# Order of ScalarE's squares and VectorE's norms in two interleaved streams of a transformer kernel

## The reference

```
x = x + softmax_over_rows(n(x) n(x)^T) n(x)            # n = layernorm
x = x + ffn(n(x))                                      # two layers
x = x + weighted_values(n(x))
x = x + ffn(n(x))                                      # the same two layers

def layer(x):                                          # one of the two, 8 heads of 64, windows of 64
    q, k, v = split(shift(x) @ wqkv)
    q = q / |q| * qs ;  k = k / |k| * ksc              # per head
    q, k = q * cos * scale + rot(q) * sin * scale, k * cos / scale + rot(k) * sin / scale
    x = x + local_attention(8 * q, k, v) @ wo          # this window and the one before
    h = layernorm(shift(x)) @ w1 + b1 ; a, g = split(h)
    return x + (a * gelu(g)) @ w2 + b2
```

## Time and profile before

| | us |
|---|---|
| median of three runs (1572.09 to 1573.59) | 1572.35 |
| the profiled execution, its own time | 1571.71 |
| its span, first to last instruction | 1569.9 |

### The profile page before, as it was taken

How to read it: one execution, slowest core, us unless ns; L and a number is a source line. 1 busy time by engine, 2 the same in 40 slices (tenths; PEclk the granted TensorE clock), 3 DMA queues, 4 the chain that set the end, 5 groups by cost and what they waited for, 6 DMA issues and landing times.

```text
span 1569.9 us, 46462 instructions
## 1 busy us (share of the span) xinstructions
PE 1445.2 (92%) x18975; PEld 1121.2 (71%) x18975; DVE 1300.5 (83%) x1692; ACT 1231.8 (78%) x1834; POOL 897.2 (57%) x626
## 2 busy tenths in 40 slices
PE   5999997889999999999998767989999999999998
PEld 3777874777777777777776554777777777777776
DVE  6777757888899999898885866988998998988884
ACT  4876867788888888888885857788888888888884
POOL 4334104666666666766761645776666666667761
PEclk9999999999999999999999878999999999999999
DMA  4312003675566756656650003666666565565562
GB/s 115 111 51 91 11 7 70 132 128 117 119 122 126 115 118 127 122 123 120 120 105 20 0 8 71 134 132 111 122 127 120 117 123 122 124 119 123 113 110 67
DMA packets 359855, 157.46 MB, mean 100 GB/s; under 512 B 299410, under 2 KB 335836, under 8 KB 359644
## 3 DMA queue, kind: packets, MB, share of 16 engines
q1 hardware_dynamic: 359644, 154.51, 49.0%
HBM read 27.29 MB, written 6.29 MB: 21 GB/s over the span
## 4 chain that ended last, share of the span: by engine, by line
PE 54%; ACT 20%; DVE 11%; issue 5%; DMA 4%; SPq 4%; POOL 1%; DVEq 0%; POOLq 0%; ACTq 0%
PE PS L199 8%; PE PS L201 7%; PE PS L200 7%; PE PS L852 6%; DMA t<-t 4%; PE PS L827 4%; PE PS L871 4%; ACT t L1059 3%; PE PS L834 3%; PE PS L860 3%; ACT t L1143 2%; PE PS L914 2%; DVE t L1256 2%; ACT L1200 2%; ACT L1143 2%
## 5 line engine op out<-in xcount | busy, mean ns | idle before, releaser
L1432 POOL TENSOR_TENSOR t<-t 128x1024 f32<-128x1024 f32 x128 | 308.2, 2408 | 207.8 <-DVE t L1262 207.4
L1438 POOL TENSOR_TENSOR t<-t 128x512 f32<-128x512 f32 x256 | 320.5, 1274 | 150.5 <-DVE t L1272 150.2
L1272 DVE TENSOR_TENSOR t<-t 128x1024 f32<-128x1024 f32 x128 | 208.5, 1629 | 0.1
L199 PE MATMUL PS<-wqh,HH 128*128 128x512 f32 x384 | 179.8, 468 | 21.0 <-DVE t L1262 10.9
L1256 DVE TENSOR_REDUCE t<-t 128x16 f32<-128x1024 f32 x128 | 156.0, 1219 | 33.3 <-ACT t L1059 32.2
L1291 DVE TENSOR_REDUCE t<-PS 128x8 bf16<-128x1024 f32 x128 | 156.1, 1220 | 16.9 <-PE PS L801 16.7
L1279 DVE TENSOR_TENSOR t<-t,PS 128x1024 bf16<-128x1024 f32 x128 | 155.1, 1212 | 9.9 <-ACT PS L1079 9.6
L1079 ACT CAST PS<-t 128x1024 f32<-128x1024 bf16 x128 | 130.2, 1017 | 41.6 <-DVE t L1291 32.2
L852 PE MATMUL PS<-t 128*64 128x65 f32 x4096 | 147.5, 224 | 13.0 <-DVE t L1325 13.0
L1262 DVE SCALAR_TENSOR_TENSOR t<-t,PS 128x1024 f32<-128x1024 f32 x128 | 155.0, 1211 | 0.6 <-ACT t L1066 0.6
L201 PE MATMUL PS<-wqh,HL 128*128 128x512 f32 x384 | 152.8, 398 | 0.0
(11 more groups left out here) (242 smaller groups left out, 3411.9 us busy)
## 6 DMA issues: line engine op xcount, KB each, us to landing
t<-t SPq DMA_DIRECT2D x254, 130.0 KB, 2.4
t<-turns SPq DMA_DIRECT2D x128, 128.0 KB, 2.8
t<-yT SPq DMA_DIRECT2D x108, 128.0 KB, 2.4
t<-t SPq DMA_TRANSPOSE x304, 3.4
t<-in_c_rope SPq DMA_DIRECT2D x32, 128.0 KB, 2.2
turns<-t SPq DMA_DIRECT2D x32, 128.0 KB, 1.9
t<-in_L_attn_a_x SPq DMA_DIRECT2D x4, 512.0 KB, 7.0
t<-yT SPq DMA_DIRECT2D x16, 127.8 KB, 2.6
```

The source lines that it names most:

```text
L199: e.matmul(o, ah, bh, start=not more, stop=False, skip_group_check=True)
L1272: e.e.tensor_tensor(BL.ta[i % 2].rearrange("p (x h) d -> p x h d", x=2), BL.qn.rearrange("p (x h) d -> p x h d", x=2), cos.to_broadcast([1 ...
L1432: e.e.tensor_tensor(BL.tc.rearrange("p (x h) d -> p x h d", x=2), BL.qn.rearrange("p (x h) d -> p x h d", x=2), sin.to_broadcast([128, 2, ...
L1438: e.e.tensor_tensor(tv[:, :, 32 * s:32 * s + 32], tv[:, :, 32 * s:32 * s + 32], BL.tc[:, :, 32 * (1 - s):32 * (1 - s) + 32], ALU.add).then ...
```

## The change

ScalarE: in every step but A, `squares(s)` is issued in front of `copy_result(s - 4)`; in A the order stays. VectorE: in G, `norms(s)` is issued in front of `rope(s - 1)`; in the others it stays behind. `normed` has one more wait, that the rotation's product of the tile before is done (`la_ta`), since otherwise nothing would keep it from overwriting `qn` early. No instruction is added or removed, and TensorE, GpSimd and SyncE keep their lists.

```diff
@@ layers_act, the loop over s
                 if on(3):
                     exps(s - 3)
+                behind_gelus = chunk_at(s, 13) is not None
+                if on(0) and not behind_gelus:
+                    squares(s)
                 if on(4):
                     copy_result(s - 4)
...
-                if on(0):
+                if on(0) and behind_gelus:
                     squares(s)
@@ layers_dve, normed(i)
                 e.wait_ge(S.la_tc, hi(i - 1) + 1)
+                e.wait_ge(S.la_ta, hi(i - 1) + 1)
@@ layers_dve, the loop over s
                 if on(2):
                     low(s - 2)
+                if on(0) and chunk_at(s, 12) is not None:
+                    norms(s)
                 if on(1):
                     rope(s - 1)
...
-                if on(0):
+                if on(0) and chunk_at(s, 12) is None:
                     norms(s)
```

## The result

| | before | after |
|---|---|---|
| median of the runs (4 and 4), us | 1572.97 (1572.09 to 1576.93) | 1557.09 (1554.27 to 1559.34) |
| ratio, 95% interval | | 0.9893 (0.9868 to 0.9918) |
| profiled execution, its own time | 1571.71 | 1558.34 |
| its span | 1569.9 | 1556.5 |
| first-layer round, us | 36.22 | 35.55 |

The forecast was 8.7 us faster; the change made it about 16 faster.

What follows compares the result with a forecast made beforehand. TensorE was taken as nearly the bound, its stalls the only gain. 16 rounds by 0.55 (8.8), ten rounds (0.5) and transposes (-0.6) made 8.7 us off 1571.71: 1563.0, as median 1563.6; range 1555.5 to 1573.

Steps and rivals of the forecast that it cites:

- both stalls of TensorE: TensorE's waits for the exps (0.44 us) and for VectorE's gated product (about 0.5), some 0.9 us a round.
- the collision: In ten second-layer rounds GpSimd's sine's product starts 0.86 us later and overlaps VectorE's cosine product, which ends 0.86 later.
- A, by G: Earlier ln, rounding and exps one step before end TensorE's stall of 0.44 us at the values; it gains 0.40.
- Bank 7 in C: TensorE's product from bank 7 waits for ScalarE's later copy; another 0.04 us lost there a round.
- The slower rival: The late copy holds TensorE's bank 7 products and the first steps: 8.7 us slower, 1581; chance 0.13.
- Its other term: In the first steps of each stage project_out (L871) passes the copy's delay on: 14 by 0.47 us, 6.6.
- B: VectorE's norms no longer wait for the squares, so TensorE's gather wins 0.19 us of its stall of 0.5.
- The second layer: Ten rounds in which late GpSimd work leaves only 0.09 less 0.04 us a round: 0.5 in all.
- The transposes (0.6): TensorE's waits in front of L816 for a transpose by L709: 0.1 us taken off, six times.
- The first 12 steps (0): Steps outside full rounds, project_out (L871) behind the later copy, norms earlier: taken as 0, between -0.3 and +0.47 us a step.
- GpSimd takes it back everywhere: Rival: GpSimd's late additions and chunk work collide in all 26 rounds, gaining only 1.3 or 2.6 us: 1570.5; chance 0.23.
- More than that: Rival: no collision in the ten rounds and a gain in the first steps, 14.3 and 2 more: 1556; chance 0.12.

Runs made afterwards that it cites:

- moving the residual: The whole change, with GpSimd's addition of the residual one step later, behind the sine's product instead of in front of it: 1555.44 us, ratio 0.9889.
- The change once more: The changed kernel run again without any edit: 1557.19 us, ratio 0.9904 to the kernel before.

## Why the prediction was right in direction and too small in size

The mechanism held: both stalls of TensorE that the forecast named were there and shrank by the path that it gave, and the loss and the collision that it expected came too. What was off is the size of one term, the reach of the collision, and a round that it took for one like the others. The runs give each term its size.

- **A, by G: right.** Forecast 0.44 won in A, less 0.04 for bank 7 in G; measured 0.44 (9.35 to 8.91) and 0.04 (10.03 to 10.07). Each link of the chain came within 0.05 us: ln 0.81 for 0.76, rounding 0.65 for 0.63, product 1.22. That the rounding would be bounded by GpSimd's additions held as well. What I hadn't worked out is how little of it is needed: ScalarE's exchange alone brings the exps 0.31 forward and 0.31 of the 0.38 that G's exchange is worth.
- **Bank 7 in C: right.** Forecast 0.04, measured 0.02 to 0.04 (C 8.15 to 8.17, and the round without it 35.55 to 35.51). The slower rival put 0.15 and 0.12 on this mechanism; it is there, at a quarter of that. (Its other term counts 14 steps outside full rounds; by the 94 exchanged steps less 78 in full rounds they are 16.)
- **B: the term was mis-sized**, 0.19 for 0.30. I took the row's idle time in front of the norms for what could be won. VectorE's instructions start some 0.08 before the end that the row of the one before gives (576.77 starts inside 575.18 + 1.67 = 576.85), so an instruction that need not wait wins the idle time and this overlap, 0.27. 0.03 is unexplained. Over 24 rounds this term is 2.6 us, and it explains the first-layer round: 0.55 forecast, 0.67 measured.
- **The second layer: the collision came, its reach was overrated.** It is there (2.46), and moving the residual gave back what it took (35.87 to 35.54). The forecast had it take all of A's gain and half of B's through `add_out`, `reduce_maxima` and `normed`, and let 0.05 a round stay. The runs show 0.38: B kept all of its 0.31, and A kept 0.11. The step that failed is "comes out about 0.1 late": `add_out` was not 0.1 late but 0.08 early. TensorE lost its time in A, at the gather that waits 0.51 for the gated product. Over some nine rounds the 0.33 more are 3 us.
- **The round of steps 12 to 15: not seen.** I counted it as a full round like the others. The wait of 1.92 in step 13 was in the trace, and the fall of the clock behind it. In the profiles the round got 1.8 and 2.7 shorter where 0.55 was forecast; 1.1 is shown without the clock, and the clock's part is observed but not explained.
- **The transposes (0.6): can't be told from the scatter. The first 12 steps (0): open.** The 5 us lost there in the first pair of profiles go with the clock and don't come back in the repeats. The thirteen executions together rather speak for a gain of some 3 us in the first stage.

Together: 14 first-layer rounds by 0.67 are 9.4, some nine and a half second-layer ones by 0.38 are 3.6, and the two rounds of steps 12 to 15 bring 3 to 5. That is 16 to 18 against 15.9 between the medians; the last of the three parts is the loose one, and the first steps are not in it. That the measured time still lies in the range owes something to luck: the range was held open downwards for a rival that had other reasons.

Of the rivals, "GpSimd takes it back everywhere" is refuted by the first layer (35.55). "More than that" had the time nearly right (1556), in the main for a wrong reason: the collision in the second layer did come. Its other reason, a gain in the first steps, stays open.

## What to carry to other kernels

A stall's worth is the distance to the start that an unhindered neighbour would have, not the idle time printed in its row. A late weight load need not show in front of its matmul: look also at the distance to the matmul behind it (0.47 for 0.43 here). An instruction that waits for two others is not freed by moving one of them forward. Moving one producer (squares before copy) may be all the gain and the second exchange beside it worth nothing or, alone, a loss: try the parts apart. Before a gain is multiplied by a count of rounds, look at the round at the seam: it had a stall four times as long and a clock of its own.

## What the runs showed of the hardware

- The 128x1024 product of VectorE and that of GpSimd, both from two SBUF operands, hardly overlap. VectorE's took 1.22 alone, 1.67 when it started 1.8 behind GpSimd's (631.95 and 633.76), and 2.46 when it started 1.04 behind (708.25 and 709.29). In both it ends 1.09 behind GpSimd's end: 635.43 and 634.34, 711.75 and 710.66. So it does where it starts 1.0 to 2.2 behind GpSimd's in the other steps of the two profiles (1.08 to 1.09). GpSimd's own product stays at 2.39 to 2.41.
- A weight load that came 0.20 late left the start of its matmul where it was (0.23 behind the one in front) and lengthened the distance to the next from 0.43 to 0.47, in every G of every kernel with the late copy; in C it is 0.26 for 0.23.
- TensorE's granted clock fell from 1.00 to between 0.54 and 0.60 behind a wait of 1.92 us, for two stretches of 2 us that the matmuls filled. The change once more had the fall in one stage and not in the other, behind the same wait of 1.86, and its round cost 1.5 us more with it (39.2 against 37.7). So the wait alone doesn't bring it about.
- Two executions of one kernel differ by 3 to 4 us in a stretch of 100 us (96.4 and 100.7 for the change), while their rounds further on agree to 0.02. The granted clock of the stretch differs with them (0.96 and 0.93). In the first pair of profiles this hid 5 of the change's 16 us.
